# LayerNorm roots moved to GpSimd, and ScalarE's order changed, in the self-attention stage of a decoder block

## The chip, the cores and the metric

The kernel runs on one core of a Trainium2 chip. The metric is the device time of one execution, in microseconds (us). A core has five engines that run their own instruction streams and meet at semaphores: TensorE (PE, its weight loads PEld), VectorE (DVE), ScalarE (ACT), GpSimd (POOL) and SyncE (SP), which here issues the DMAs.

## What is computed

A decoder block: `x + attention(layernorm(x))`, then the same with cross-attention, then with a mixture of experts. The change touches the first of the three, causal self-attention with 16 heads over 16 sequences of 224 rows and 512 columns, whose softmax is replaced by a rational function:

```python
def rational_softmax(scores, eps=EPS):
    num = 0.5 * (1.0 + scores * jax.lax.rsqrt(1.0 + scores * scores))
    return num / (jnp.sum(num, axis=-1, keepdims=True) + eps)
...
def _layernorm(x, axis=-1, eps=1e-05):
    m = jnp.mean(x, axis=axis, keepdims=True)
    v = jnp.var(x, axis=axis, keepdims=True)
    return (x - m) / jnp.sqrt(v + eps)
```

## The kernel before

The stage works in NIT = 8 iterations of two sequences (448 rows, four tiles of 112). An iteration has NG = 8 slots, and a slot handles one group of four heads of one sequence. The bodies are called first (i = 0), second (1), mid (2 to 6, a loop) and last (7). Nothing is scheduled by a tool: each engine's `body` writes its instructions slot by slot, and a table `PLAN` says which matrix products (units) PE computes beside the attention in each slot. Precise products are made of float32 numbers split into a high and a low part, so every operand has a high part (ACT copies it) and a low part (DVE subtracts).

In slot s:

- **PE** (L853) makes `scores(s + 1)` (L799 to L815), then `values(s)` (L819 to L835, which waits for the weights' two halves and for `o_made` of slot s - 1), then the slot's units. Slot 0 has Q3, a transpose, OUT2 and OUT3; slot 1 has K3, V2, V3 and the transpose T1c0; slots 2, 3 and 4 are light (Z0 and Z1; Z2; Z3 and OUT0, and a transpose each); slots 5, 6 and 7 have three products each. OUT2 waits for `o_lo` of all eight slots of the iteration before. Products alternate between two PSUM banks.
- **ACT** (L690) takes the high part of the output of slot s - 1 (`hi_of_output`, L660), then `roots(s + 1)`: a square of the scores (L641), a reciprocal root (L643), a square (L645). Then `reciprocal(s)`, copies of PE's products out of PSUM (`evacuate`), and `off_diagonal(s + 1)` (L649). The square waits for the scores and for `y_made` of the slot before, since it overwrites what DVE then reads.
- **DVE** (L551) makes the low part of the output of slot s - 1 (L509), then `product_signed(s + 1)` (L486) and `numerator(s + 1)` (L490, L493, L495; `y_made` comes from L493), then `output(s)` (L501, L502, L504; it sets `o_made`), then low parts of transposes, residuals and LayerNorm statistics.

The two LayerNorms of an iteration, half 0 (the next rows of x) and half 1 (rows after attention), have their root in three pieces: DVE's statistics (`mv_made`), ACT's reciprocal root of four numbers per row (`root_of`, L597, 0.28 us) and five tiny DVE instructions that refine it (`refine`, L467 to L475). ACT then normalises the four tiles (`normalise`, L602). For half 0 the root is in slot 0 and the tiles are in slot 1, for half 1 they are in slots 1 and 2. Half 0's tiles are what T1c0 transposes in slot 1. SP loads the next rows and stores Z0 after half 1's tiles are done (`xn_made[1]`). POOL does nothing in the eight iterations.

Of the kernel before, what the change touches and what calls it, by code (L numbers as in the profile page):

```python
# [11 lines left out]
R = T // 2  # L12
TPI = 4
# [113 lines left out]
def self_attention(nc, ctx, block, handover, x, w_qkvT, w_outT, w_qT, slopes, x1_dram, q2_dram):  # L127
# [51 lines left out]
    nt = [sb(f"nt{k}", [R, 2, TPI]) for k in range(2)]  # L179
# [26 lines left out]
    newton = [sem("newton0"), sem("newton1")]  # L206
    rstd_made = [sem("rstd_made0"), sem("rstd_made1")]
# [86 lines left out]
    CONSTS = 6  # L294

# [86 lines left out]
    def _(pool):  # L382
# [15 lines left out]
        for a in range(2):  # L398
# [9 lines left out]
                           base=0, channel_multiplier=1).then_inc(const_ready, 1)  # L408

    @block.vector  # L410
    def _(dve):
# [177 lines left out]
        refine(1, NIT - 1)  # L589
# [4 lines left out]
    def _(act):  # L594
        def root_of(half, n):
            act.wait_ge(mv_made[half], n * TPI + TPI)
            act.activation(rstd[half][:], mv[half][:, :, 1], ACT.Abs_reciprocal_sqrt, bias=eps[0:R, 0:1]).then_inc(root_made[half], 1)  # L597

        def normalise(half, n, src, dst):
            act.wait_ge(rstd_made[half], n + 1)  # L600
            for j in range(TPI):
                ins = act.activation(dst[:, j, :], src[:, j, :], ACT.Identity, bias=shift[half][:, j:j + 1],  # L602
                                     scale=rstd[half][:, j:j + 1])
            ins.then_inc(xn_made[half], 1)
# [58 lines left out]
        root_of(0, 0)  # L663
# [15 lines left out]
        root_of(0, 1)  # L679
# [10 lines left out]
        def body(i, kind):  # L690
            for s in range(NG):
                if s > 0:
# [31 lines left out]
        root_of(1, NIT - 1)  # L724
# [1178 lines left out]
```

## Time and profile before

| | us |
|---|---|
| median of 3 runs (3229.09, 3233.4, 3235.1) | 3233.4 |
| the profiled execution, its own time | 3229.13 |
| its span, first to last instruction | 3227.3 |
| self-attention stage, until about | 765 |
| of an iteration (slot 0 at 304.55 to the next at 388.86) | 84.31 |

PE was busy 94% of the span, DVE 51%, ACT 42%, POOL 22%; the mean granted clock was 0.97. In the first stage PE is busy for 644.2 of 765 us and DVE for 584.4. A matmul's record has a modelled end, so a PE without gaps is read from its starts. Idle time in brackets in a row is that of the engine just before the instruction, with what ended it. In the names, `a_ew` holds the scores' work tiles, `a_o_sb` the output, `a_oTh` and `a_oTl` its high and low part.

### The profile page before, as it was taken

The page shows a single profiled execution, that of the slowest core. Times are in us where ns is not written, and L with a number is a line of the kernel's source. Part 1 is how long each engine was busy: PE and PEld are TensorE (multiplying, and loading weights), DVE is VectorE, ACT ScalarE, POOL GpSimd, SP SyncE. Part 2 cuts the span into 40 slices and gives each one's busy share as a digit, 9 for nine tenths or more (in the row PEclk, how much of TensorE's full clock was granted, in tenths as well). Part 3 has the DMA queues.
Part 4 walks back from the last instruction along what each step waited for, and adds up shares of the span by engine and source line. Part 5 has one row for each costly group of instructions (what it writes and reads, how often), then busy time and mean ns, then how long its engine had stood idle before and what let it go on. Part 6 is the DMA issues. An engine that isn't in the chain of part 4 may idle for free. (4 is left out here: it accounts for less than half of the span.)

```text
span 3227.3 us, 50841 instructions
## 1 busy us (share of the span) xinstructions
PE 3018.3 (94%) x19312; PEld 2477.8 (77%) x19312; DVE 1646.6 (51%) x3608; ACT 1348.0 (42%) x2298; POOL 700.2 (22%) x721
## 2 busy tenths in 40 slices
PE   5889998978999999999999949999999999999997
PEld 4667777756788777778777738888888888888886
DVE  5888888873556556666566633333333333333321
ACT  5677777764555555555555511111111111111111
POOL 0000000011111221112121033243434343434332
PEclk9889999989999999999999969999999999999999
DMA  3011111123111111111111022141313131313122
GB/s 100 24 35 44 37 45 45 46 82 121 42 50 38 45 38 56 51 38 42 41 52 34 25 74 75 54 97 55 96 55 96 56 95 56 95 57 94 57 71 37
DMA packets 93875, 189.72 MB, mean 59 GB/s; under 512 B 17568, under 2 KB 27552, under 8 KB 91712
## 3 DMA queue, kind: packets, MB, share of 16 engines
q1 hardware_dynamic: 79168, 158.68, 16.1%
q0 software_dynamic: 14592, 29.43, 5.1%
q8 instruction: 82, 1.34, 0.2%
q14 instruction: 33, 0.27, 0.0%
HBM read 140.25 MB, written 47.82 MB: 58 GB/s over the span
## 5 line engine op out<-in xcount | busy, mean ns | idle before, releaser
L1777 ACT ACTIVATE f_hf<-f_h 128x448 f32<-128x448 f32 x256 | 139.4, 544 | 1014.1 <-PE f_h L1804 958.0
L1748 DVE CAST f_hh<-f_hf 128x448 fp32r<-128x448 f32 x256 | 105.9, 414 | 847.0 <-ACT f_hf L1777 822.0
L1819 PE MATMUL f_y<-f_w2h,f_hh 128*128 128x512 f32 x896 | 357.5, 399 | 0.0
L1819 PE MATMUL f_y<-f_w2h,f_hl 128*128 128x512 f32 x896 | 354.0, 395 | 0.0
L1819 PE MATMUL f_y<-f_w2l,f_hh 128*128 128x512 f32 x896 | 352.2, 393 | 0.0
L1707 POOL TENSOR_TENSOR f_w1l<-f_raw,f_w1h 128x512 fp32r<-128x512 f32 x128 | 182.4, 1425 | 778.6 <-DVE f_w1h L1731 778.5
L1396 ACT ACTIVATE c_s_sb<-c_s_sb,c_nmx 112x750 f32<-112x750 f32 x256 | 236.1, 922 | 159.6 <-DVE c_nmx L1239 156.6
L1388 ACT COPY c_pT<-psum 125x672 f32<-125x672 f32 x256 | 184.6, 721 | 224.3 <-PE psum L1496 223.2
L1804 PE MATMUL f_h<-f_xTh,f_w1h 128*128 128x448 f32 x1024 | 255.2, 371 | 2.9 <-DVE f_xTl L1736 1.4
L1496 PEld LDWEIGHTS psum<-a_ident,c_s_sb 112*125 112x125 f32 x1536 | 193.5, 189 | 79.9 <-issue 76.2
L1804 PE MATMUL f_h<-f_xTl,f_w1h 128*128 128x448 f32 x1024 | 250.7, 366 | 0.0
L1804 PE MATMUL f_h<-f_xTh,f_w1l 128*128 128x448 f32 x1024 | 249.7, 365 | 0.0
L1235 DVE CUSTOM_DVE_ANT_0 c_s_sb<-psum,c_mb 112x750 f32<-112x750 f32 x256 | 238.5, 932 | 0.0
L1496 PE MATMUL psum<-a_ident,c_s_sb 112*125 112x112 f32 x1536 | 221.4, 280 | 6.5 <-ACT c_pT L1388 6.5
L1804 PEld LDWEIGHTS f_h<-f_xTh,f_w1h 128*128 128x128 f32 x1024 | 188.3, 188 | 50.8 <-DVE f_xTl L1736 23.2
L1487 PE MATMUL psum<-h_kT,h_q 64*112 64x376 f32 x1024 | 196.9, 502 | 13.1 <-DVE c_mx L1235 11.9
L1804 PEld LDWEIGHTS f_h<-f_xTh,f_w1l 128*128 128x128 f32 x1024 | 193.0, 189 | 16.8
L1804 PEld LDWEIGHTS f_h<-f_xTl,f_w1h 128*128 128x128 f32 x1024 | 192.8, 188 | 16.5
L1819 PEld LDWEIGHTS f_y<-f_w2h,f_hl 128*128 128x128 f32 x896 | 168.2, 188 | 39.6
L1819 PEld LDWEIGHTS f_y<-f_w2l,f_hh 128*128 128x128 f32 x896 | 169.0, 189 | 29.6
L1819 PEld LDWEIGHTS f_y<-f_w2h,f_hh 128*128 128x128 f32 x896 | 168.3, 188 | 29.3
L1191 POOL DMA_INDIRECT table_dram<-c_pay,c_slotu x64 | 61.9, 967 | 539.4 <-DVE c_slotu L1318 524.8
(252 smaller groups left out, 5766.6 us busy)
## 6 DMA issues: line engine op xcount, KB each, us to landing
f_raw<-in_w SPq DMA_DIRECT2D x128, 512.0 KB, 4.2
h_craw<-in_ctxT SPq DMA_DIRECT2D x16, 1125.0 KB, 5.1
a_x_in<-in_x SPq DMA_DIRECT2D x9, 896.0 KB, 5.5
a_xr<-in_x SPq DMA_DIRECT2D x8, 896.0 KB, 6.0
x_dram<-a_xr SPq DMA_DIRECT2D x8, 896.0 KB, 4.8
q_dram<-a_q SPq DMA_DIRECT2D x32, 224.0 KB, 5.4
h_q<-q_dram SPq DMA_DIRECT2D x16, 448.0 KB, 5.4
c_x<-x_dram SPq DMA_DIRECT2D x16, 448.0 KB, 4.9
```

Source lines behind the costliest of these rows:

```text
L1191: pool.indirect_dma_start(out=table_dram, out_offset=bass.IndirectOffsetOnAxis(ap=slotu[:, q:q + 1], axis=0), in_=pay[:, q, :], in_offset= ...
L1235: nc.vector.tensor_tensor_reduce(out=half(s_sb[:, h % 4, :]), in0=score_view(h), in1=half(mb[:]), scale=1.0, scalar=-FLT_MAX, op0=ALU.add, ...
L1388: act.copy(probs_view(h), pt_view).then_inc(p_copied, 1)
L1396: act.activation(s_sb[:, h % 4, :], s_sb[:, h % 4, :], ACT.Exp, bias=nmx[:, h:h + 1], accum_out=den[:, h:h + 1]).then_inc(e_made, 1)
L1487: mm = pe.matmul(scb[e][0:R, a, 0:HW], q[rows, m, t0:t0 + R], kT[rows, m, j0:j0 + HW], start=True, stop=True, tile_position=(64 * e, 0))
L1496: mm = pe.transpose(ptb[0:JB, 128 * j:128 * j + R], s_sb[:, h % 4, JB * j:JB * j + JB], ident[:])
L1707: pool.tensor_tensor(w1s[1][:, l % NSLOT].rearrange("p k c -> p (k c)"), raw1[:, g % 2, l % 2, :], w1s[0][:, l % NSLOT].rearrange("p k c - ...
L1748: dve.tensor_copy(hs[0][:, l % 2, c * HC:c * HC + HC], hf[:, c, :]).then_inc(h_hi, 1)
L1777: act.activation(hf[:, c, :], H[:, 0:HC], ACT.Gelu_apprx_tanh).then_inc(free, 1)
L1804: mm = pe.matmul(H[:, 0:HC], w1s[a][:, l % NSLOT, k, :], xT[l // FB % 2][b][:, k, c * HC:c * HC + HC], start=q + k == 0, stop=(q, k) == (2 ...
L1819: mm = pe.matmul(Y[t][:], hs[a][:, l % 2, 128 * t:128 * t + 128], w2s[b][:, l % NSLOT, :], start=j == 0 and q == 0, stop=last_of_expert(l) ...
```

## The change

The three pieces of each root become one chain of 14 tiny instructions on POOL, an initial guess by bit arithmetic and two steps of refinement, each waiting for the one before. `root_of` and `refine` leave the loops of ACT and DVE. Half 0's four tiles are normalised at the end of slot 0, half 1's at the ends of slots 1 and 2, two and two, each behind `off_diagonal`. ACT computes `roots(s + 1)` ahead of `hi_of_output(s - 1)`, and DVE makes `product_signed(s + 1)` ahead of the output's low part. The start of the stage and its end keep the old root.

```diff
+        def root_of_variance(half, use, mv_count, used_count):
...
+            pool.wait_ge(mv_made[half], mv_count)
+            pool.sem_inc(chain_seen, 1)
...
+            then(pool.tensor_scalar(var, mv[half][:, :, 1], LN_EPS, None, ALU.add))
+            then(pool.tensor_scalar(rows.bitcast(I32), var.bitcast(I32), -0.5, float(0x5f3759df), ALU.mult, ALU.add))
+            then(pool.tensor_tensor(square, rows, rows, ALU.mult))
+            then(pool.tensor_tensor(product, square, var, ALU.mult))
...
+            pool.tensor_scalar(shift[half][:], product, -1.0, None, ALU.mult).then_inc(rstd_made[half], 1)
+
+        def body(i, kind):
+            if kind in ("second", "mid"):
+                root_of_variance(0, i - 1, i * TPI + 2 * TPI, i + 1)
+            if kind != "first":
+                root_of_variance(1, i - 1, i * TPI, i - 1 if kind != "second" else None)
...
@@ DVE, body
                 late = [u for u in units(kind, s - 1, 1) if u[0] == "T"] if s > 0 else []
+                for unit in late:
+                    lo_of_transpose(i, kind, unit)
+                if has_step(kind, s + 1):
+                    product_signed(*step(i, s + 1))
                 if s > 0:
                     lo_of_output(i, s - 1)
                 elif kind != "first":
                     lo_of_output(i - 1, NG - 1)
-                for unit in late:
-                    lo_of_transpose(i, kind, unit)
                 if has_step(kind, s + 1):
-                    product_signed(*step(i, s + 1))
                     numerator(*step(i, s + 1))
-                if s == 0 and kind in ("second", "mid"):
-                    refine(0, i + 1)
-                if s == 1 and kind != "first":
-                    refine(1, i - 1)
                 output(i, s)
...
@@ ACT, body
+                if has_step(kind, s + 1):
+                    roots(*step(i, s + 1))
                 if s > 0:
                     hi_of_output(i, s - 1)
                 elif kind != "first":
                     hi_of_output(i - 1, NG - 1)
-                if has_step(kind, s + 1):
-                    roots(*step(i, s + 1))
-                if s == 0 and kind in ("second", "mid"):
-                    root_of(0, i + 1)
-                if s == 1 and kind != "first":
-                    root_of(1, i - 1)
                 reciprocal(i, s)
...
-                if s == 1 and kind in ("second", "mid"):
-                    normalise(0, i + 1, x_in, x_in)
-                if s == 2 and kind != "first":
-                    normalise(1, i - 1, xr, xn2)
                 if has_step(kind, s + 1):
                     off_diagonal(*step(i, s + 1))
+                if s == 0 and kind in ("second", "mid"):
+                    normalise(0, i + 1, x_in, x_in)
+                if s in (1, 2) and kind != "first":
+                    normalise(1, i - 1, xr, xn2, 2 * s - 2, 2 * s - 1)
                 for unit in late[1:]:
                     evacuate(i, kind, unit)
```

How the instructions stand, in the loop over the mid iterations. First ACT, from the end of slot 0 (the last instruction of `roots` is the row before these) into slot 1, before:

```order
L597 ACTIVATE a_rstd_102<-a_mv_100,a_eps 112x4 [waits a_mv_made0]
L653 ACTIVATE a_rden<-psum,a_eps 128x224 [waits a_pv_full]
L655 ACTIVATE a_rden<-a_rden 128x224 [waits a_rs_made]
L624 ISA
L626 ACTIVATE a_qT<-psum 128x448 [waits a_gen_full]
L609 CAST a_x2Th<-psum 128x448 [waits a_t_full]
L649 ACTIVATE a_ew<-a_ew 112x4x112 [waits a_y_made]
L660 CAST a_oTh<-a_o_sb 128x224 [waits a_o_made]
L637 REGISTER_ALU
L641 ACTIVATE a_ew<-psum 112x1344 [waits a_y_made,a_s_full]
```

and now, the same stretch:

```order
L701 CAST a_oTh<-a_o_sb 128x224 [waits a_o_made]
L694 ACTIVATE a_rden<-psum,a_eps 128x224 [waits a_pv_full]
L696 ACTIVATE a_rden<-a_rden 128x224 [waits a_rs_made]
L665 ISA
L667 ACTIVATE a_qT<-psum 128x448 [waits a_gen_full]
L650 CAST a_x2Th<-psum 128x448 [waits a_t_full]
L690 ACTIVATE a_ew<-a_ew 112x4x112 [waits a_y_made]
L640 REGISTER_ALU
L642 ACTIVATE a_x_in<-a_x_in,a_shift_106,a_rstd_102 112x512 [waits a_rstd_made0]
L642 ACTIVATE a_x_in<-a_x_in,a_shift_106,a_rstd_102 112x512 x3
L678 REGISTER_ALU
L682 ACTIVATE a_ew<-psum 112x1344 [waits a_y_made,a_s_full]
```

The output's high part has left the place ahead of the next square, and four normalised tiles have come there, which wait for POOL's chain.

Second DVE, the head of slot 0, before:

```order
L509 TENSOR_TENSOR a_oTl<-a_o_sb,a_oTh 128x224 [waits a_o_hi]
L485 ISA
L486 TENSOR_TENSOR a_ew<-psum,a_ew 112x1344 [waits a_r_made]
L490 SCALAR_TENSOR_TENSOR a_ew<-a_ew 112x1344 [waits a_rr_made]
L493 SCALAR_TENSOR_TENSOR a_ew<-a_ew 112x1344 [waits a_m_made,a_p_made]
L495 SCALAR_TENSOR_TENSOR a_ew<-a_ew,a_keep 112x4x224 [waits a_y_made]
L466 REGISTER_ALU
L467 TENSOR_TENSOR a_nt_104<-a_rstd_102 112x4 [waits a_root_made0]
```

and now:

```order
L529 TENSOR_TENSOR a_ew<-psum,a_ew 112x1344 [waits a_r_made]
L551 ISA
L552 TENSOR_TENSOR a_oTl<-a_o_sb,a_oTh 128x224 [waits a_o_hi]
L533 SCALAR_TENSOR_TENSOR a_ew<-a_ew 112x1344 [waits a_rr_made]
L536 SCALAR_TENSOR_TENSOR a_ew<-a_ew 112x1344 [waits a_m_made,a_p_made]
L538 SCALAR_TENSOR_TENSOR a_ew<-a_ew,a_keep 112x4x224 [waits a_y_made]
L543 REGISTER_ALU
L544 SCALAR_TENSOR_TENSOR a_dt<-psum,a_rden 128x224 [waits a_rden_made]
```

The low part, which OUT2 waits for, now stands behind the product of the next slot, and ahead of the instruction that sets `y_made`; the refinement is gone.

## Rows read from the trace of the kernel before

**Rows 1.** One iteration, busy time: us, each engine, granted clock, DMA share, GB/s
```profile
304.55:388.86 84.31, 77.29 (x689) 60.89 (x688) 69.89 (x103) 62.07 (x90) 0.00 (x0) 0.96 0.16 44
```
**Rows 2.** Waits in 100 to 600 us: us in total, times, longest
```profile
ACT a_oTh L660 <- DVE a_o_sb L504: 42.4, 24, 2.5
PE psum L832 <- DVE a_o_sb L504: 25.7, 12, 4.4
```
**Rows 3.** PE's timeline, first, third and fourth iteration: start, length, row, idle before
```profile
107.62 0.59 PE L832 MATMUL psum<-a_ew,a_v 112*32 112x224 f32 x8 [1.70 <-DVE a_o_sb L504]
...
264.30 0.58 PE L832 MATMUL psum<-a_ew,a_v 112*32 112x224 f32 x8 [1.81 <-DVE a_o_sb L504]
...
304.55 0.46 PE L807 MATMUL psum<-a_qT,a_kT 32*112 32x112 f32 x8
...
309.59 1.15 PE L737 MATMUL psum<-a_wouth,a_oTh 128*112 128x512 f32 x4
...
338.80 0.93 PE L832 MATMUL psum<-a_ew,a_v 112*32 112x224 f32 x8 [3.05 <-ACT a_ew L649]
...
348.62 0.58 PE L832 MATMUL psum<-a_ew,a_v 112*32 112x224 f32 x8 [2.91 <-DVE a_o_sb L504]
...
358.54 0.59 PE L832 MATMUL psum<-a_ew,a_v 112*32 112x224 f32 x8 [0.27 <-DVE a_o_sb L504]
```
**Rows 4.** ACT's and DVE's timeline in its slot 4
```profile
348.79 1.28 ACT L641 ACTIVATE a_ew<-psum 112x1344 f32<-112x1344 f32 x1
...
351.56 1.56 DVE L486 TENSOR_TENSOR a_ew<-psum,a_ew 112x1344 f32<-112x1344 f32 x1 [2.25 <-ACT a_ew L643]
353.03 1.55 DVE L490 SCALAR_TENSOR_TENSOR a_ew<-a_ew 112x1344 f32<-112x1344 f32 x1
354.69 1.56 DVE L493 SCALAR_TENSOR_TENSOR a_ew<-a_ew 112x1344 f32<-112x1344 f32 x1
356.28 0.58 ACT L649 ACTIVATE a_ew<-a_ew 112x448 f32<-112x448 f32 x1 [1.07 <-DVE a_ew L493]
...
358.71 1.28 ACT L641 ACTIVATE a_ew<-psum 112x1344 f32<-112x1344 f32 x1
```
**Rows 5.** Statistics of half 0, squares of slots 1 to 3, tiles of half 1
```profile
306.61 0.38 DVE L462 BATCH_NORM_AGGREGATE a_mv<-a_stats 112x2 f32<-112x6 f32 x4
...
316.48 1.28 ACT L641 ACTIVATE a_ew<-psum 112x1344 f32<-112x1344 f32 x1
...
328.14 1.29 ACT L641 ACTIVATE a_ew<-psum 112x1344 f32<-112x1344 f32 x1
...
335.32 2.92 ACT L602 ACTIVATE a_work<-a_xr,a_shift,a_rstd 112x512 f32<-112x512 f32 x4
...
338.88 1.28 ACT L641 ACTIVATE a_ew<-psum 112x1344 f32<-112x1344 f32 x1
```
**Rows 6.** The second stage: its chain of roots on POOL, DVE beside it
```profile
1009.73 0.22 POOL L1168 TENSOR_SCALAR c_nt<-c_mv 112x2 f32<-112x2 f32 x1 [4.32 <-DVE c_mv L1254]
...
1010.95 0.61 DVE L1225 TENSOR_SCALAR c_s_sb<-c_s_sb,c_rec 112x750 f32<-112x750 f32 x1
1011.27 0.36 POOL L1172 TENSOR_SCALAR c_nt<-c_nt 112x2 f32<-112x2 f32 x1 [0.20 <-POOL c_nt L1171]
...
1013.71 0.19 POOL L1178 TENSOR_SCALAR c_nt<-c_nt 112x2 f32<-112x2 f32 x1 [0.20 <-POOL c_nt L1177]
```
**Rows 7.** POOL beside DVE in the last iteration; durations min/median/max in ns
```profile
L94 POOL TENSOR_TENSOR h_wvl<-h_stage,h_wvh x3: 1272/1278/1441, 704.7 to 707.4; 128x512 fp32r<-128x512 f32 x3
...
705.30 0.95 DVE L504 SCALAR_TENSOR_TENSOR a_o_sb<-a_dt 128x224 f32<-128x224 f32 x1
...
L504 DVE SCALAR_TENSOR_TENSOR a_o_sb<-a_dt x64: 391/391/1653, 64.8 to 729.3; 128x224 f32<-128x224 f32 x64
```
**Rows 8.** Granted clock (third number from the end) in slot 4, two iterations
```profile
350.00:355.00 5.00, 5.00 (x31) 4.19 (x24) 3.34 (x3) 4.31 (x7) 0.00 (x0) 0.74 0.00 0
...
265.00:270.00 5.00, 5.00 (x43) 4.21 (x35) 2.76 (x2) 4.90 (x7) 0.00 (x0) 1.00 0.04 6
```

More of the change, by code:

```diff
@@ L178, in self_attention @@
     rstd = [sb(f"rstd{k}", [R, TPI]) for k in range(2)]
-    nt = [sb(f"nt{k}", [R, 2, TPI]) for k in range(2)]
+    nt = [sb(f"nt{k}", [R, 3, TPI]) for k in range(2)]
     shift = [sb(f"shift{k}", [R, TPI]) for k in range(2)]
@@ L206, in self_attention @@
     newton = [sem("newton0"), sem("newton1")]
+    chain, chain_seen = [sem("chain0"), sem("chain1")], sem("chain_seen")
     rstd_made = [sem("rstd_made0"), sem("rstd_made1")]
@@ L294, in self_attention @@
     CONSTS = 6
+    CHAIN = 13
     QKV_DEAD = (gen_full, product_number(NIT - 1, "last", "V3") + 1)
@@ L408, in _, with then @@
                            base=0, channel_multiplier=1).then_inc(const_ready, 1)
+        def root_of_variance(half, use, mv_count, used_count):
+            var, square, product = (nt[half][:, k, :] for k in range(3))
+            rows = rstd[half][:]
+            done = [0]
+            def then(ins):
+                done[0] += 1
+                ins.then_inc(chain[half], 1)
+                pool.wait_ge(chain[half], use * CHAIN + done[0])
+                pool.sem_inc(chain_seen, 1)
+            pool.wait_ge(mv_made[half], mv_count)
+            pool.sem_inc(chain_seen, 1)
+            if used_count is not None:
+                pool.wait_ge(xn_made[half], used_count)
+                pool.sem_inc(chain_seen, 1)
+            then(pool.tensor_scalar(var, mv[half][:, :, 1], LN_EPS, None, ALU.add))
+            then(pool.tensor_scalar(rows.bitcast(I32), var.bitcast(I32), -0.5, float(0x5f3759df), ALU.mult, ALU.add))
+            then(pool.tensor_tensor(square, rows, rows, ALU.mult))
+            then(pool.tensor_tensor(product, square, var, ALU.mult))
+            then(pool.tensor_scalar(square, product, -10 / 3, None, ALU.add))
+            then(pool.tensor_tensor(square, square, product, ALU.mult))
+            then(pool.tensor_scalar(square, square, 5.0, 3 / 8, ALU.add, ALU.mult))
+            then(pool.tensor_tensor(rows, square, rows, ALU.mult))
+            then(pool.tensor_tensor(square, rows, rows, ALU.mult))
+            then(pool.tensor_tensor(product, square, var, ALU.mult))
+            then(pool.tensor_scalar(product, product, -0.5, 1.5, ALU.mult, ALU.add))
+            then(pool.tensor_tensor(rows, product, rows, ALU.mult))
+            then(pool.tensor_tensor(product, mv[half][:, :, 0], rows, ALU.mult))
+            assert done[0] == CHAIN
+            pool.tensor_scalar(shift[half][:], product, -1.0, None, ALU.mult).then_inc(rstd_made[half], 1)
[4 more added lines that the diff above has]
+                root_of_variance(1, i - 1, i * TPI, i - 1 if kind != "second" else None)
+        iterations(pool, body)
     @block.vector
@@ L594, in _, with root_of, normalise @@
     def _(act):
-        def root_of(half, n):
-            act.wait_ge(mv_made[half], n * TPI + TPI)
+        def root_of(half, count):
+            act.wait_ge(mv_made[half], count * TPI)
             act.activation(rstd[half][:], mv[half][:, :, 1], ACT.Abs_reciprocal_sqrt, bias=eps[0:R, 0:1]).then_inc(root_made[half], 1)
-        def normalise(half, n, src, dst):
+        def normalise(half, n, src, dst, *js):
             act.wait_ge(rstd_made[half], n + 1)
-            for j in range(TPI):
+            for j in js or range(TPI):
                 ins = act.activation(dst[:, j, :], src[:, j, :], ACT.Identity, bias=shift[half][:, j:j + 1],
                                      scale=rstd[half][:, j:j + 1])
-            ins.then_inc(xn_made[half], 1)
+            if j == TPI - 1:
+                ins.then_inc(xn_made[half], 1)
         def hi_of_transpose(i, kind, unit):
@@ L662, in _ @@
         act.wait_ge(const_ready, CONSTS)
-        root_of(0, 0)
+        root_of(0, 1)
         for k in range(KC):
@@ L678, in _ @@
         roots(0, 0)
-        root_of(0, 1)
+        root_of(0, 2)
         for unit in ("V0", "V1"):
```

4 lines of the change are left out of this document (2 added, 2 removed).

## Prediction

> **What bounds the kernel now.** I read the busy times of one iteration first [rows 1]. Of 84.3 us PE is busy 77.3 and DVE 69.9: neither fills it, so the order of waits decides, slot by slot. The waits say where [rows 2]: ACT sits 42 us of 500 ahead of the output's high part, which waits for DVE, and PE 26 us ahead of `values`, for the same DVE instruction. Then PE's timeline [rows 3]: in the fourth iteration (i = 3, slot 0 at 304.55) PE waits 3.05 us in slot 3, 2.91 in slot 4 and 0.27 in slot 5, that is in and behind the light slots. In slots 5, 6, 7 and 0 it runs without a gap, and there the scores come so late that nothing ACT does sooner helps. So there are two regimes: heavy slots go by PE, light slots by a ring through ACT and DVE. I count all times from slot 0 of an iteration; the ring runs from the start of one square (call it R) to the next.
>
> **The ring, before and after.** In slot 4 one turn is 348.79 to 358.71, 9.92 us [rows 4]: square and root until DVE's product starts, 2.77; to the first half of the numerator 1.47; to its second half 1.66; to `y_made` 1.59; then the off-diagonal copy beside 0.8 us of DVE's third part and output, the output's high part, and the next square. The change takes the wait for the output out. ACT's next square then waits for `y_made` and the off-diagonal copy ahead of it, 0.5 us. But DVE's low part now stands inside the ring: it needs ACT's high part, which follows the third of the roots (product start + 1.33 + 0.38, less overlap), so it starts 1.66 us after the product did and takes 0.30: the numerator begins 0.5 us later than today. New turn: 2.77 + 1.96 + 1.65 + 1.59 + 0.52 = 8.5 us, 1.4 less. `o_made`, which PE's next `values` waits for, comes at R + 10.1; today it is R + 9.7 (348.79 to 358.5). So what one slot gives, the half microsecond takes back once at the end of the light stretch.
>
> **Removed from DVE and ACT.** Five refinements per half, some 0.2 us each, 2 us of DVE per iteration; ACT's 0.3 us root. In heavy slots DVE and ACT are idle beside PE and this is worth nothing; in slot 1 it takes 0.9 us from the way to `o_made`.
>
> **Added: the chain on POOL.** The nearest rows are the second stage's chain [rows 6]: the first instruction at 1009.73, the eleventh at 1013.71, less the 0.17 that one of them was held, so 0.38 us a step. Fourteen steps take 5.15 us when nobody disturbs them. Half 0's statistics are made at 2.4 (306.61 + 0.38 - 304.55) [rows 3, 5]; the half microsecond on DVE makes it 2.9, and the chain starts at 3.1. Undisturbed it ends at 8.3, before the tiles want it (off-diagonal copy done at 9.5).
>
> It will be disturbed. In the second stage a chain step of 0.19 us took 0.36, since a DVE instruction with 0.61 us was running: it ended 0.07 us after DVE's did [rows 6]. In the last iteration DVE's L504, whose two inputs both lie in SBUF, took 0.95 and once 1.65 us where its median is 0.39, both times beside POOL's subtractions, and one of POOL's three took 1441 ns where the others took 1272 and 1278 [rows 7]. So one of the two engines stands while the other runs, and it goes both ways. The Trainium skill states this ("SBUF — State Buffer", section "SBUF: two separate sides"): VectorE and GpSimd share a port pair under an exclusive lock, which a VectorE instruction with two SBUF inputs takes against a GpSimd instruction that reads SBUF. The trace agrees, by the 1441 ns and the 1.65 us. In this stage L490, L493 and L495 have two SBUF inputs and stand back to back for 4.2 us (the first two in [rows 4], the third is 1.09 long); L486 has one in PSUM and took nobody's time.
>
> Step by step: product at 3.8; by the low part's end, 5.8, eight steps are done. The ninth waits for L490 and ends at 7.5, the tenth for L493 (9.1), the eleventh for L495 (10.2), the twelfth at 10.6, the thirteenth behind L504 (11.3), the last at 11.7. The chain takes 8.6 us, not 5.15. My bounds are 8.3 (no holding) and 12.5 (POOL loses each turn to DVE's next instruction and only goes on behind L495); I take 11.7, because rows 6 and 7 both show the waiting engine getting its turn at the other's end.
>
> **Moved: the tiles of half 0.** ACT, done with the off-diagonal copy at 9.5, waits 2.1 us for the chain; four tiles are 2.92 [rows 5], of which 2.85 pass before the next. The square of slot 1 starts at 14.55. Today it starts at 11.93 (316.48) [rows 5], so the slot begins 2.6 us late, and queued behind the tiles on ACT are that square and PE's copies.
>
> From there by the new terms. `y_made` is R + 7.97 = 22.5; off-diagonal copy, two tiles of half 1 (1.4), a copy of V3 and of T1c0 (0.9): slot 2's square at 25.4; today 23.6. Half 1's chain starts at 15.0, runs mostly beside L486, ends by 22.7 and is not waited for. Slot 2: `y_made` 33.4, copy 0.5, two tiles 1.4: slot 3's square at 35.3; today 34.3. PE's `values` in slot 3 wait for `o_made` at 25.4 + 10.1 = 35.5; today 34.25. Slot 4: 35.3 + 10.1 = 45.5; today 44.1. `xn_made[1]` comes at 35.4, today 33.7: SP's queue behind it (next rows, the stores of Z0 to Z2) shifts by 1.7, and ACT's copy of Z2, which waits for Z0's store, starts at 42.5, so slot 4's square starts at 43.9, today 44.2. Slot 5's `values` start at the later of two: the ring's 43.9 + 10.1 = 54.0, and PE's own way through slot 4. Today they start at 53.99. PE's own way is 1.1 later (45.5 against 44.1, less the 0.27 it waits today) if PE runs slowly in slot 4, and earlier than 54.0 if it does not. In the iteration shown the granted clock over 5 us of slot 4 was 0.74, after a wait of 2.91 us; an iteration earlier it was 1.00, after 1.81 [rows 3, 8]. Full is 2.4 GHz, the lower level 1.2. Three of the five mid iterations are of the first kind. So a mid iteration costs 0 to 1.1 more: five make **+3.2**.
>
> **OUT2.** The output's low part of slot 7, the last that OUT2 waits for, now stands behind slot 0's product: it is there at 5.9, and OUT2 wants it at 5.04 (309.59) [rows 3]. PE waits 0.9 us in slot 0. In mid iterations this hides, since slot 1's square comes later than PE does, at 14.55 against 12.7. If the chain were fast it would still hide, because the tiles end at 12.4.
>
> **First, second, last.** In the first iteration there are no tiles and PE has little to do, so the ring is shortened without a price: PE's wait of 1.70 in slot 5 [rows 3] goes, and with the 1.4 us per turn in slots 3 and 4 it comes out **-2.3**, less what slots 5 to 7 of 10.0 us give back. The second pays the late tiles as a mid one does: **+0.8**. The last has no tiles of half 0 and gains in its light slots, with the loads that it waits for in slot 2 unmoved in kind: **-1.1**. Stages two and three are not touched.
>
> **Sum.** -2.3 + 0.8 + 3.2 - 1.1 = +0.6 us against the profiled execution's own 3229.1: 3229.7. That execution was 4.3 below the median of the runs, so on the median's scale about **3234 us**. A measurement of this kernel can tell about 0.2%, 6.5 us, from no change.
>
> **Rivals.**
>
> *The ring gets free* (chance 0.19). POOL's small steps slip between DVE's, or wait only for a short part of each. For it: no row shows a short POOL step beside L490 itself. Against: rows 7. The chain ends at 8.3, slot 1's square at 12.4, everything behind is 2.1 us earlier than above: a mid iteration gains 1.1 to 2.1, first and second 3.6, last 1.1: 12 us in all, 3221.
>
> *PE keeps its clock in the light slots* (0.05). If the waits of about 3 us fell under 2, as in the third iteration, slots 3 and 4 would lose nothing: up to 2 us an iteration beyond the above, some 14 us in all, 3220. Against: the waits worked out above are 3.2 and 3.1, not shorter.
>
> *The chain is the new bound* (0.18), on the other side. POOL gets no turn from L490 to L495 and DVE is in turn held by POOL's steps, 0.4 us a numerator. Slot 1's square then starts at 15.4 and the numerator is longer: 1.2 more in each of six iterations, 7 us, 3241. It decides from the point where the chain ends later than 9.5, since from there each us of it is one of ACT's. For it: the chain is 8.6 us in a gap of 6.4. Against: the two-way turns in rows 7.
>
> Main case, within 0.2%: 0.58. With a rest for clocks and runs: faster 0.24, same 0.58, slower 0.18. The range reaches from the free ring (3221) and the kept clock (3220) to the bound chain and its scatter, 3242.
>
> **What would show it.** In the page of the changed kernel: POOL steps in the first stage with a mean well over 0.2 us, up to 1.5 under L490 and L493; ACT waiting about 2 us for POOL ahead of the four tiles (if it waits under 0.3, the first rival holds); PE waiting about 0.9 us for `a_oTl` ahead of OUT2; ACT's wait for L504 ahead of the high part gone; squares 8.5 us apart in slots 3 and 4 of the first iteration; a mid iteration of 84.3 to 85.4 us. If it is under 83 or over 86 I am wrong, and the place is slot 1's square, at 14.55.

## The result and the profile after

| | before | after |
|---|---|---|
| median of the runs, us (12 each, same chip) | 3229.98 | 3238.44 |
| lowest and highest | 3227.68 to 3236.79 | 3236.76 to 3242.31 |
| profiled execution: time, span | 3229.1, 3227.3 | 3237.24, 3235.5 |
| granted clock, mean of the span | 0.970 | 0.968 |

The ratio is 1.0024, interval [1.0015, 1.0033]: the change costs 8 us. The time lies in the range, but not where the forecast put it (no difference within 0.2%): it is slower by a little more than that. A ratio is good to about 3 us either way, here and in the experiments below (4 us where a kernel had five to seven runs).

Where the 8.2 us between the two spans lie. The marks are the starts of the squares of each iteration's first group (L641 before, L682 after):

| stretch | before | after | difference | forecast |
|---|---|---|---|---|
| up to the first square | 40.88 | 41.33 | +0.4 | 0 |
| first iteration | 86.87 | 84.38 | -2.5 | -2.3 |
| second | 83.07 | 84.41 | +1.3 | +0.8 |
| five mid iterations | 422.51 | 425.34 | +2.8 | +3.2 |
| last, to its last square | 83.16 | 85.45 | **+2.3** | **-1.1** |
| from there to the second stage's first scores | 51.22 | 52.24 | +1.0 | 0 |
| second and third stage | 2459.59 | 2462.35 | **+2.8** | **0** |

The first three terms of the forecast are met within 0.6 us. The last iteration is missed by 3.4 us and the later stages by 2.8.

Waits of the kernel after, 100 to 600 us (columns: who waits, for whom; us in total, times, longest), the answer to [rows 2]:

```profile
DVE a_ew L529 <- ACT a_ew L684: 75.8, 46, 2.8
...
ACT a_ew L690 <- DVE a_ew L536: 49.2, 38, 2.4
PE psum L869 <- DVE a_o_sb L547: 37.6, 22, 4.3
...
ACT a_x_in L642 <- POOL a_shift L443: 13.9, 6, 2.4
...
PE psum L774 <- ACT a_kT L669: 5.6, 6, 1.1
PE psum L774 <- DVE a_oTl L552: 4.9, 6, 1.1
```

ScalarE's 42 us ahead of the output's high part are gone from the list. Its wait ahead of the off-diagonal copy, also for VectorE, has grown by 24 us; before, it was

```profile
ACT a_ew L649 <- DVE a_ew L493: 25.3, 27, 2.2
```

New are ScalarE's wait for the chain, PE's for the low part ahead of OUT2 (both forecast), and one that the prediction gave no price: PE waits for ScalarE's copy of K, which stands behind the late tiles.

GpSimd's chain of half 0 in the fourth iteration, VectorE beside it, and PE at OUT2 with ScalarE at the tiles (timeline after; start, duration), the answer to [rows 4, 5]:

```profile
307.17 0.23 POOL L429 TENSOR_SCALAR a_nt<-a_mv 112x4 f32<-112x4 f32 x1 [64.76 <-DVE a_mv L505]
...
308.74 0.22 POOL L433 TENSOR_SCALAR a_nt<-a_nt 112x4 f32<-112x4 f32 x1 [0.20 <-POOL a_nt L432]
309.14 0.20 POOL L434 TENSOR_TENSOR a_nt<-a_nt 112x4 f32<-112x4 f32 x1 [0.18 <-POOL a_nt L433]
309.54 0.33 POOL L435 TENSOR_SCALAR a_nt<-a_nt 112x4 f32<-112x4 f32 x1 [0.20 <-POOL a_nt L434]
310.06 1.29 POOL L436 TENSOR_TENSOR a_rstd<-a_nt,a_rstd 112x4 f32<-112x4 f32 x1 [0.18 <-POOL a_nt L435]
311.52 1.48 POOL L437 TENSOR_TENSOR a_nt<-a_rstd 112x4 f32<-112x4 f32 x1 [0.18 <-POOL a_rstd L436]
313.18 0.95 POOL L438 TENSOR_TENSOR a_nt<-a_nt 112x4 f32<-112x4 f32 x1 [0.18 <-POOL a_nt L437]
...
315.73 0.23 POOL L443 TENSOR_SCALAR a_shift<-a_nt 112x4 f32<-112x4 f32 x1 [0.20 <-POOL a_nt L441]
```
```profile
307.80 1.56 DVE L529 TENSOR_TENSOR a_ew<-psum,a_ew 112x1344 f32<-112x1344 f32 x1 [0.98 <-ACT a_ew L684]
309.43 0.39 DVE L552 TENSOR_TENSOR a_oTl<-a_o_sb,a_oTh 128x224 fp32r<-128x224 f32 x1
309.74 1.55 DVE L533 SCALAR_TENSOR_TENSOR a_ew<-a_ew 112x1344 f32<-112x1344 f32 x1
311.39 1.56 DVE L536 SCALAR_TENSOR_TENSOR a_ew<-a_ew 112x1344 f32<-112x1344 f32 x1
312.98 1.09 DVE L538 SCALAR_TENSOR_TENSOR a_ew<-a_ew,a_keep 112x896 f32<-112x896 f32 x1
```
```profile
309.96 1.15 PE L774 MATMUL psum<-a_wouth,a_oTh 128*112 128x512 f32 x4 [0.77 <-DVE a_oTl L552]
...
312.98 0.58 ACT L690 ACTIVATE a_ew<-a_ew 112x448 f32<-112x448 f32 x1 [1.96 <-DVE a_ew L536]
315.99 2.94 ACT L642 ACTIVATE a_x_in<-a_x_in,a_shift,a_rstd 112x512 f32<-112x512 f32 x4 [2.43 <-POOL a_shift L443]
318.83 1.27 ACT L682 ACTIVATE a_ew<-psum 112x1344 f32<-112x1344 f32 x1
```

Beside L529, which has an input in PSUM, a step of the chain takes about 0.20 us. Beside L533, L536 and L538, whose inputs all lie in SBUF, it takes 1.29, 1.48 and 0.95, and each of the three ends 0.05 or 0.06 us after VectorE's instruction. So the chain advances one step per VectorE instruction, and VectorE pays nothing that shows: the 13 times that L533 (L490 before) ran beside a chain it took 1549 to 1552 ns, the other 51 times 1546 to 1554. ScalarE waits 2.43 us, and slot 1's square starts 14.9 us after slot 0 (303.92, where PE's scores begin, to 318.83); forecast 14.55.

The last iteration, where the forecast had a gain (the chain of half 1, then ScalarE in slot 1):

```profile
659.88 0.23 POOL L429 TENSOR_SCALAR a_nt<-a_mv 112x4 f32<-112x4 f32 x1 [76.94 <-DVE a_mv L505]
...
668.64 0.23 POOL L443 TENSOR_SCALAR a_shift<-a_nt 112x4 f32<-112x4 f32 x1 [0.20 <-POOL a_nt L441]
```
```profile
668.90 1.52 ACT L642 ACTIVATE a_work<-a_xr,a_shift,a_rstd 112x512 f32<-112x512 f32 x2 [2.81 <-POOL a_shift L443]
670.33 0.56 ACT L671 COPY a_v<-psum 112x512 f32<-112x512 f32 x1
670.79 1.29 ACT L682 ACTIVATE a_ew<-psum 112x1344 f32<-112x1344 f32 x1
```

Half 1's chain, "not waited for" in the mid iterations, is waited for here: there are no late tiles of half 0 that would hold ScalarE up for as long. Slot 1's square to slot 2's takes 13.24 us where it took 10.80.

### The profile page after: what moved, and what is told of

It is laid out like the page before. It is cut to its first block and busy times, and to the rows that moved or that the text cites. A ratio compares the mean times of both kernels' runs of the same rounds, so it can differ in the third digit from the quotient of the medians.

```text
span 3235.5 us, 51170 instructions
## 1 busy us (share of the span) xinstructions
PE 3024.1 (93%) x19312; PEld 2479.4 (77%) x19312; DVE 1643.1 (51%) x3543; ACT 1345.1 (42%) x2285; POOL 772.8 (24%) x903
## 5 line engine op out<-in xcount | busy, mean ns | idle before, releaser
L1841 PEld LDWEIGHTS f_h<-f_xTh,f_w1h 128*128 128x128 f32 x1024 | 188.5, 188 | 51.2 <-DVE f_xTl L1773 23.5
L1524 PE MATMUL psum<-h_kT,h_q 64*112 64x376 f32 x1024 | 198.0, 505 | 13.5 <-DVE c_mx L1272 12.3
```

What stands on the lines that cost most here:

```text
L1524: mm = pe.matmul(scb[e][0:R, a, 0:HW], q[rows, m, t0:t0 + R], kT[rows, m, j0:j0 + HW], start=True, stop=True, tile_position=(64 * e, 0))
L1841: mm = pe.matmul(H[:, 0:HC], w1s[a][:, l % NSLOT, k, :], xT[l // FB % 2][b][:, k, c * HC:c * HC + HC], start=q + k == 0, stop=(q, k) == (2 ...
```

## Experiments

Twelve kernels. "Against before" is the ratio of medians to the kernel before, run beside it on the same chip. The chips differ between groups of runs, so medians of different groups are compared by these ratios. In the tables a **step n** is the time from slot n's square to the next slot's, in a mid iteration (the fifth, i = 4, unless two values are given).

### The parts one by one

`ring_only`: the kernel before, with this on ScalarE and, on VectorE, `lo_of_output` moved behind `product_signed` in the same way.

```
+                if has_step(kind, s + 1):
+                    roots(*step(i, s + 1))
                 if s > 0:
                     hi_of_output(i, s - 1)
                 elif kind != "first":
                     hi_of_output(i - 1, NG - 1)
-                if has_step(kind, s + 1):
-                    roots(*step(i, s + 1))
```

> The kernel before with one part of the change: roots ahead of the output's high part on ScalarE, the signed product ahead of the output's low part on VectorE. Roots by ScalarE and VectorE and the tiles' places as before. Theory 1 (late tiles cost what the shorter ring gives): without the late tiles the ring's gain stays. First iteration -2.3, each of the seven others about -1 in slots 3 and 4, so 6 to 10 us under the kernel before: about 3222, and a mid iteration of 83.2 to 83.8. Theory 2 (the ring takes back what it gives, since o_made comes at R + 10.1 where it was R + 9.7, and PE's clock falls): within 3 us of the kernel before, a mid iteration of 84.3 to 84.9.

`chain_only`: the kernel before with `root_of_variance` on GpSimd for both halves, and `root_of` and `refine` taken out of the iterations:

```
+        def body(i, kind):
+            if kind in ("second", "mid"):
+                root_of_variance(0, i - 1, i * TPI + 2 * TPI, i + 1)
+            if kind != "first":
+                root_of_variance(1, i - 1, i * TPI, i - 1 if kind != "second" else None)
...
-                if s == 0 and kind in ("second", "mid"):
-                    refine(0, i + 1)
-                if s == 1 and kind != "first":
-                    refine(1, i - 1)
```

> The kernel before with another part alone: both roots by GpSimd's chain of 14 steps, orders and the tiles' places as before. Theory 1: the chain ends 8.6 us after its start, at about 11.4 for half 0 and 23 for half 1, ahead of tiles wanted at about 17 and 28, so nobody waits for it; DVE loses nothing by the turns: 0 to 5 us under the kernel before. Theory 2 (DVE is held in turn, 0.4 us a numerator beside a chain): 4 to 7 us above it, and L490, L493 (as numbered before) with means 0.2 or more above their medians in slots 0 and 1.

`tiles_back`: the changed kernel with

```
+                if s == 1 and kind in ("second", "mid"):
+                    normalise(0, i + 1, x_in, x_in)
+                if s == 2 and kind != "first":
+                    normalise(1, i - 1, xr, xn2)
                 if has_step(kind, s + 1):
                     off_diagonal(*step(i, s + 1))
-                if s == 0 and kind in ("second", "mid"):
-                    normalise(0, i + 1, x_in, x_in)
-                if s in (1, 2) and kind != "first":
-                    normalise(1, i - 1, xr, xn2, 2 * s - 2, 2 * s - 1)
```

> The changed kernel with the tiles at their old places: half 0's four in slot 1, half 1's four in slot 2, ahead of the off-diagonal copy. Theory 1 (ScalarE's wait of 2.4 us for the chain and the tiles in slot 0 are what costs): slot 1's square starts at 12 and not 14.9, a mid iteration is 83 to 84 us, the whole 8 to 16 us under the changed kernel. Theory 2 (the wait is hidden by PE as the heavy slots are PE's): within 3 us of the changed kernel.

`last_old`: the changed kernel with

```
-                if s in (1, 2) and kind != "first":
+                if s in (1, 2) and kind in ("second", "mid"):
                     normalise(1, i - 1, xr, xn2, 2 * s - 2, 2 * s - 1)
+                if s == 2 and kind == "last":
+                    normalise(1, i - 1, xr, xn2)
```

> The changed kernel, except that in the last iteration alone half 1's four tiles stand together in slot 2. Theory 1 (the last iteration's loss is ScalarE's wait of 2.81 us for half 1's chain in slot 1): slot 1 is 10.4 to 10.8 us instead of 13.2, the whole 2 to 3.5 us under the changed kernel. Theory 2 (the loads of h_stage and xr hold slot 2 anyway): under 1 us, slot 2 longer by what slot 1 is shorter.

| | median, us | against before | step 0 | step 1 | step 2 | step 3 | step 4 | step 5 |
|---|---|---|---|---|---|---|---|---|
| before | | 1 | 10.83 | 11.65 | 10.74 | 9.91 | 9.93 | 10.40 |
| ring_only | 3227.92 | 0.9992 [0.9983, 1.0001] | 11.62 | 11.71 | 10.46 | 8.42 | 11.42 | 10.42 |
| chain_only | 3233.13 | 1.0005 [0.9996, 1.0014] | 10.62 | 11.71 | 10.77 | 9.92 | 9.92 | 10.37 |
| tiles_back | 3231.37 | 1.0002 [0.9993, 1.0011] | 11.68 | 11.72 | 10.46 | 8.42 | 11.39 | 10.46 |
| last_old | 3236.51 | 1.0018 [1.0009, 1.0027] | 13.80 | 10.72 | 9.86 | 8.66 | 9.62 | 11.15 |
| after | 3238.44 | 1.0024 [1.0015, 1.0033] | 13.81 | 10.72 | 9.85 | 8.42 | 11.49 | 10.46 |

The parts add up within the intervals: ring and chain alone give 0.9992 and 1.0005, both with the tiles at their old places 1.0002. What is left, 1.0024 against 1.0002, is the tiles' move: 7 us, nearly the whole loss. `tiles_back` is nearer theory 1, but short of its 8 to 16 us below the changed kernel. Its mid iterations are 83.9 to 85.1 us, one of five under 84, and slot 1's square starts 12.8 us after slot 0, not 12: with the tiles gone from there, PE's wait ahead of OUT2 is bare.

`ring_only` is nearer theory 2: 2.4 us under the kernel before, and its mid iterations are 84.9 to 86.0 us (before: 84.3, once 85.2), while its first iteration gained 2.6. Two things take the ring's gain back. Step 0 is 0.8 to 0.9 longer, in every iteration but the first: PE's wait ahead of OUT2,

```profile
PE psum L738 <- DVE a_oTl L509: 4.9, 6, 1.1
```

(waits of `ring_only`, 100 to 600 us). And step 4 is longer: 11.4 us, in two of the five 12.4, for 9.9. Windows of i = 2 and 3, one line per step 3 and step 4 (columns: window, length, busy us and instructions of PE, PEld, DVE, ACT, POOL, granted clock, DMA share, GB/s):

```profile
251.94:260.36 8.42, 5.31 (x68) 4.28 (x68) 5.55 (x6) 6.47 (x10) 0.00 (x0) 1.00 0.63 165
260.36:272.74 12.38, 10.60 (x84) 8.05 (x88) 10.61 (x16) 6.52 (x11) 0.00 (x0) 0.72 0.24 59
...
337.96:346.37 8.41, 6.81 (x68) 5.51 (x68) 5.59 (x6) 6.47 (x10) 0.00 (x0) 0.80 0.65 172
346.37:357.80 11.43, 9.65 (x84) 7.71 (x88) 10.54 (x16) 6.47 (x11) 0.00 (x0) 0.85 0.24 54
```

PE still waits in the light slots, 3.05 us in slot 3 for the off-diagonal copy and 3.2 to 4.7 in slot 4 for the output, and around slot 4 its clock is at the lower level for a while. Before, that time lay in a step that the ring made 9.92 long anyway: there, too, PE was busy 9.65 of 9.92 us at a mean clock of 0.83. With a ring of 8.42 the step behind is PE's own: 84 matmuls take 9.65 at a mean clock of 0.85 and 10.60 at 0.72, and the step follows. In `tiles_back` the same step was 9.87 and 9.68 in two iterations where PE ran at 1.00 in it (the slower stretch lay in slot 3), and 11.39 to 11.46 in the other three, at 0.85. Step 5 gives a part back: it is 10.4 behind a slow step 4 and 10.9 to 11.1 behind a fast one. That the clock sets the length of step 4 is read from such rows; no run changes the clock alone.

`chain_only` answers the third rival. The chain at its old places is waited for by nobody, and steps 0 to 5 are as before, step 0 even 0.2 shorter (the refinements). Theory 2, VectorE held, is out: no step in the table is longer by more than 0.06. Yet the run is no faster (its interval reaches from 1.3 us faster to 4.5 slower); that is taken up below.

`last_old`: slot 1's square to slot 2's is 10.41 in the last iteration (13.24 after), as theory 1 says, and from that iteration's slot 0 to its last square it takes 72.0 us where the changed kernel takes 75.0, so slot 2 does not take it back. The whole is 1.9 us less, just under the 2 to 3.5 expected and too little to tell from the scatter; the step itself is what shows it.

### OUT2's wait, and the low part's place

`slot0_old`: `ring_only` with, on ScalarE,

```
+                if s == 0 and kind != "first":
+                    hi_of_output(i - 1, NG - 1)
                 if has_step(kind, s + 1):
                     roots(*step(i, s + 1))
                 if s > 0:
                     hi_of_output(i, s - 1)
-                elif kind != "first":
-                    hi_of_output(i - 1, NG - 1)
```

and the same for `lo_of_output` and `product_signed` on VectorE.

> The run ring_only, except that slot 0 alone keeps the old order on both engines (high part ahead of the roots, low part ahead of the product). In ring_only slot 0's square to slot 1's square took 11.68 where before it took 10.83. Theory 1 (the 0.85 is PE's wait ahead of OUT2 for the low part, no longer covered by late tiles): that step is 10.83 again in seven iterations, and the whole 4 to 6 us under ring_only, about 3222. Theory 2 (the light slots wait for the output anyway and PE's clock falls for as long): the 0.85 comes back in slots 3 to 5, within 2 us of ring_only.

`lo_late`: in addition, on VectorE:

```
                 if has_step(kind, s + 1):
                     product_signed(*step(i, s + 1))
+                if s == 4:
-                if s > 0:
                     lo_of_output(i, s - 1)
                 if has_step(kind, s + 1):
                     numerator(*step(i, s + 1))
...
                 output(i, s)
+                if s not in (0, 4):
+                    lo_of_output(i, s - 1)
```

> The run slot0_old, and the output's low part on VectorE goes behind output's three instructions in slots 1, 2, 3, 5, 6 and 7 (in slot 4, where OUT0 wants it, it stays behind the product). Theory 1 (from a square to the output was 10.19 because the low part and the late product stand in it): it is about 9.3, the wait of PE ahead of values in slots 3 and 4 is some 0.5 to 0.9 shorter, and the whole 3 to 8 us under slot0_old. Theory 2 (PE's way through slot 4 at its lower clock decides): within 2 us of slot0_old.

`tb_lo_late`: the orders of `lo_late` put into `tiles_back`.

> The same orders as lo_late, with GpSimd's chains and the tiles at their old places. Theory 1 (the chain is worth nothing where nobody waits for it, as chain_only at 3233 against 3230): within 3 us of lo_late. Theory 2 (without refinements on VectorE slot 1's output comes sooner, and it is that which the shorter ring can use): 3 us or more under lo_late.

`late_fixed`: the orders of `lo_late` put into the changed kernel, tiles late as they are.

> The changed kernel, chain and late tiles as they are, with the orders of lo_late (slot 0 as before the change, the output's low part behind the output in six slots). Theory 1 (the late tiles and the wait for the chain cost the same 7 us in any order): about 3225, 7 above tb_lo_late, with slot 0's square to slot 1's at 13.5 to 13.8. Theory 2 (with the output sooner PE has room, and the late tiles are hidden): within 3 us of tb_lo_late, 3218.

| | median, us | against before | step 0 | step 1 | step 3 | step 4 | mid iterations, us |
|---|---|---|---|---|---|---|---|
| slot0_old | 3224.57 | 0.9972 [0.9961, 0.9983] | 10.63 | 11.86 | 8.41 | 9.95 | 83.0 to 84.2 |
| lo_late | 3216.55 | 0.9952 [0.9938, 0.9965] | 10.63 | 11.87 | 7.96 | 11.42 | 82.9 to 85.0 |
| tb_lo_late | 3218.34 | 0.9956 [0.9942, 0.9969] | 10.62 | 11.71 | 8.31 | 9.53 | 82.7 to 84.7 |
| late_fixed | 3234.39 | 1.0011 [1.0002, 1.0019] | 13.72 | 11.52 | 8.23 | 11.14 | 83.5 to 85.4 |

`slot0_old`: the wait for `a_oTl` is gone from the list and step 0 back at 10.6; 0.9972 against `ring_only`'s 0.9992 is 6.5 us. Theory 1. `lo_late`: 6.5 us more by the ratios, which is theory 1 by the time, though by half of what was expected in the rows: from slot 3's square to the output that PE waits for it is 9.7 us and not 10.2 (9.3 was expected), PE's wait in slot 4 is 1.6 or 2.7 us in four iterations of five (4.2 in one) where `slot0_old` has 2.0 or 3.1, and that in slot 3, for the off-diagonal copy, is 3.05 as it was. It beats the kernel before by 15 us and the changed one by 23, with no root moved. `tb_lo_late` is within 2 us of it, less than the scatter: where nobody waits for it, the chain is worth nothing that can be measured (theory 1).

`late_fixed` met neither theory: 1.0011 against 0.9956 is 18 us, not 7 and not 3, though slot 0's square to slot 1's is 13.5 to 13.7, as theory 1 has it. With OUT2's wait gone PE only arrives sooner at the next: its products in slot 1 want a bank that ScalarE frees with K's copy, and that stands behind the tiles and a square. PE's timeline in slot 1, i = 3:

```profile
318.26 1.08 PE L776 MATMUL psum<-a_wqkvh,a_xTl 128*112 128x512 f32 x4
321.13 1.23 PE L776 MATMUL psum<-a_wqkvh,a_xTh 128*112 128x512 f32 x4 [1.79 <-ACT a_kT L671]
322.16 1.91 PE L776 MATMUL psum<-a_wqkvl,a_xTh 128*112 128x512 f32 x4
323.87 1.86 PE L776 MATMUL psum<-a_wqkvh,a_xTl 128*112 128x512 f32 x4
```

The wait is 1.79 us (1.0 in the changed kernel), and behind it four matmuls take 1.9 us instead of 1.08: the lower clock. In a mid iteration where the clock stayed up, step 1 took 10.26; in the four others 11.52. That is a part of the 18 us: in the profiled executions the two kernels' mid iterations differ by 1.6 us on the mean, and the first stage by 13.6 us; the later stages of that execution of `late_fixed`, the fastest of its twelve, are 3.4 shorter. The rest is not followed.

### The price of waiting for the chain

`short_chain`: the changed kernel without the last refinement,

```
-    CHAIN = 13
+    CHAIN = 9
...
-            then(pool.tensor_tensor(square, rows, rows, ALU.mult))
-            then(pool.tensor_tensor(product, square, var, ALU.mult))
-            then(pool.tensor_scalar(product, product, -0.5, 1.5, ALU.mult, ALU.add))
-            then(pool.tensor_tensor(rows, product, rows, ALU.mult))
```

> The changed kernel with four of the chain's fourteen steps left out, the second refinement of the root: the roots are coarser, nothing else differs. Theory 1 (ScalarE's wait of 2.4 us for the chain is on the path of slot 0): the wait is under 0.5, slot 0's square to slot 1's is 11.7 to 12.4 and not 13.8, and the whole 4 to 10 us under the changed kernel. Theory 2 (the late tiles alone cost what they cost, by PE's copies behind them): within 2 us of the changed kernel.

3231.03 us, 0.9998 [0.9989, 1.0007]: 8 us under the changed kernel by the ratios. Step 0 is 12.01 (13.81), ScalarE waits 0.6 us at most (under 0.5 was expected; waits, 100 to 600 us):

```profile
ACT a_x_in L638 <- POOL a_shift L439: 3.1, 5, 0.6
```

Theory 1. The 1.8 us that step 0 gets back are worth 2.2 in the second iteration, 2.4 in the last (half 1's chain: 11.45 for 13.24) and 0.3 to 2.2, 0.9 on the mean, in a mid one, where step 1 takes up the rest (11.49 for 10.72).

This and `tiles_back` say together what the late tiles cost. Steps 0 and 1 of a mid iteration sum to 22.5 us before, 24.5 in the changed kernel, 23.5 in `short_chain` with the tiles late, and 23.4 in `tiles_back` with the whole chain. So of the 2 us one is ScalarE's wait for the chain. The other is PE's wait ahead of OUT2, which `ring_only` has too (23.3 to 23.4) and `slot0_old` not (22.5). The tiles' new place by itself costs nothing as long as that wait stands beside them.

### Why the second stage is longer

In `chain_only` the first stage got 1.5 us shorter between first and last square, and the kernel did not get faster. That is within its interval, but the second stage has a loss of the same size that repeats. In the second stage the twelve periods from the 25th scores to the 121st (the matmuls of L1487 before) took 816.2 to 816.5 us in the five kernels without the chain (`ring_only`, `slot0_old`, `lo_late` and the two below), and 817.8 to 818.6 in all seven with it (before: 817.7, with two longer steps of another kind, told below). The difference comes in equal pieces, 0.13 us in each period, at one place: the fifth of a period's eight intervals between scores is 6.45 instead of 6.32. The kernel `lo_late`, then `tb_lo_late`, there (timeline, start and duration):

```profile
1002.46 0.19 ACT L1399 ACTIVATION_READ_ACCUMULATOR c_s_sb<-c_s_sb,c_nmx 112x1 f32 x1
...
1002.70 0.19 POOL L1181 TENSOR_SCALAR c_nt<-c_nt 112x2 f32<-112x2 f32 x1 [0.20 <-POOL c_nt L1180]
1002.77 0.16 DVE L1226 RECIPROCAL c_rec<-c_den 112x1 f32<-112x1 f32 x1 [1.18 <-PE psum L1499]
```
```profile
1002.77 0.19 ACT L1435 ACTIVATION_READ_ACCUMULATOR c_s_sb<-c_s_sb,c_nmx 112x1 f32 x1
...
1003.02 0.19 POOL L1217 TENSOR_SCALAR c_nt<-c_nt 112x2 f32<-112x2 f32 x1 [0.20 <-POOL c_nt L1216]
...
1003.22 0.16 DVE L1262 RECIPROCAL c_rec<-c_den 112x1 f32<-112x1 f32 x1 [1.31 <-PE psum L1535]
```

ScalarE and GpSimd stand to each other as before; VectorE's reciprocal starts 0.20 after GpSimd's step instead of 0.07. Nothing of this stage was edited. Three kernels asked what else moved. `wide_nt` and `more_sems` are `lo_late` with one of these each:

```
-    nt = [sb(f"nt{k}", [R, 2, TPI]) for k in range(2)]
+    nt = [sb(f"nt{k}", [R, 3, TPI]) for k in range(2)]
...
+    chain, chain_seen = [sem("chain0"), sem("chain1")], sem("chain_seen")
```

`dve_shift` is `tb_lo_late` with

```
+        for cell in cells:
+            dve.memset(cell, 0.0)
         dve.wait_ge(x_loaded, 16)
```

with 34 one-column places of `stats[1]`, `mv[1]` and `shift[1]` as `cells`.

> The run lo_late with the scratch of both roots one row larger, as in the change, and not used. In every run with GpSimd's chain in the first stage the second stage is longer: one RECIPROCAL of VectorE per period starts 0.19 us after a GpSimd step began, at that step's end, where without the chain it starts 0.06 after it; the period is 0.13 longer, some 2 us over the stage. Theory 1 (the places of the second stage's tensors in SBUF, which the larger scratch moves, decide it): 0.19 here as well. Theory 2 (it is not the places): 0.06 and the period of lo_late.

> The run lo_late with the three semaphores of the change allocated and not used, so that the second stage's semaphores have other numbers. Theory 1 (the numbers decide the 0.13 us): the reciprocal starts 0.19 after the GpSimd step. Theory 2: 0.06, as in lo_late, and what is left is GpSimd's own program.

> The run tb_lo_late (GpSimd's chain, tiles at their old places, orders of lo_late) with 34 small memsets at VectorE's very start, where it waits for its first load. The chain took 34 instructions out of VectorE's program ahead of the second stage's loop and put 88 into GpSimd's; the memsets put VectorE's loop back at the count it has before the change. Theory 1 (where VectorE's loop lies in its program decides the 0.13 us by which the RECIPROCAL of every period starts late): it starts 0.06 after the GpSimd step again, and the second stage, from the first scores to the 126th, is 1066 us and not 1068.4; the whole 1 to 3 us under tb_lo_late. Theory 2 (it is GpSimd's program, or that both engines take part): 0.19 as before, and the time of tb_lo_late within 1.5 us.

`wide_nt`, a single execution: 3212.49 us, reciprocal 0.06 after the step, twelve periods in 816.2. `more_sems`, a single execution: 3212.87 us, 0.07 and 816.3. So it is neither the tensors' places nor the semaphores' numbers. `dve_shift`: 3219.94 us, 0.9947 [0.9933, 0.9960] (its chip ran the kernel before at 3238.17, so the ratio counts; it is not to be told from `lo_late`'s and `tb_lo_late`'s).

```profile
999.01 0.19 POOL L1220 TENSOR_SCALAR c_nt<-c_nt 112x2 f32<-112x2 f32 x1 [0.20 <-POOL c_nt L1219]
999.07 0.17 DVE L1265 RECIPROCAL c_rec<-c_den 112x1 f32<-112x1 f32 x1 [1.18 <-PE psum L1538]
```

0.06 again, and the 0.13 is gone from every period: with GpSimd's chain and its program unchanged, 34 instructions ahead of VectorE's loop undo it. That is theory 1 for the place; how a loop's place acts on this one instruction no run shows. Its times were not met: 1071.4 us to the 126th scores, not 1066, since in nine of the twelve periods another interval, which is 9.22 in `lo_late`, took 9.84 to 9.89, so that this kernel's twelve periods are the longest of all, 822.1. Before has two such, `tb_lo_late` none. What makes that one come and go stays open.

Because of its two, the profiled kernel before takes 817.7 us for the twelve periods and the changed one 817.8: the 0.13 us are no part of the +2.8 in the table above. Of that, 1.2 us lie ahead of the 25th scores, 1.4 between the 126th and the last, and 0.3 behind. Among the fourteen kernels' profiles the first stretch takes 204.8 to 208.4 and the second 14.6 to 17.4, so a single pair says nothing of a cause there. Not tried: shifting GpSimd's program alone.

## Why the prediction was right where it was, and wrong where not

**The chain's length: right, with one step miscounted.** Forecast 8.6 us from start to end; measured 8.79 (307.17 to 315.96). It ended 12.04 us after slot 0, forecast 11.7 with bounds of 8.3 and 12.5. The mechanism is the one argued from [rows 6, 7]: a step runs to the end of VectorE's instruction and gets its turn there. The Trainium skill ("SBUF — State Buffer", section "SBUF: two separate sides") calls the shared port pair an exclusive lock that holds for a whole instruction, and the rows agree: about 0.20 us beside an input in PSUM, 1.29 and 1.48 beside two in SBUF. The turn between two VectorE instructions is in the rows. What the prediction had wrong is "by the low part's end, 5.8, eight steps are done": from 3.1 on, eight steps of 0.38 us end at 6.1, so seven are done. The trace has seven, and the eighth (L436) waits where the ninth was expected. That one step is the 0.34 us by which the chain ended late. The first rival (a free ring) is out, the chain is 8.8 us and not 5.15. Half of the third (VectorE held 0.4 us a numerator) is out too: L533 beside a chain takes what it takes without.

**Slot 1's square and the squares behind it: right.** Forecast, counted from slot 0: 14.55, 25.4, 35.3, 43.9; measured 14.9, 25.7, 35.5, 44.3. `values` of slots 3, 4 and 5: forecast 35.5, 45.5 and 54.0 to 55.1, measured 35.9, 45.7 and 54.5. The waits: ScalarE 2.1 forecast, 2.43 measured; OUT2 0.9 forecast, 0.77.

**The mid iterations: right in sum, with the shares a little off.** +3.2 forecast, +2.8 measured; 84.4 to 85.6 each, forecast 84.3 to 85.4. The bound of 0 to 1.1 for PE's clock was the right form: the steps 4 of 9.5 to 9.9 (clock 1.00) and of 11.3 to 11.5 (0.85) are the two cases. But two iterations were of the slow kind and not three, at 85.6, and the three fast ones were 84.4 to 84.9 and not 84.3. That these two misses cancel is luck.

**OUT2: right here, wrong in what was said of it in general.** The text says the wait would hide even with a fast chain, since the tiles end at 12.4. By its own numbers it would not quite: PE comes at 12.7. In `short_chain`, where ScalarE still waits 0.6 us, slot 1's square starts at 13.12 and PE's scores are ready at 12.75, so it hides by 0.4. It hides only behind the late tiles: in `tiles_back` PE's scores set the square, at 12.8. There the same wait costs about 1 us an iteration: 0.9992 to 0.9972 for removing it.

**The last iteration: the failed step.** "The last has no tiles of half 0 and gains in its light slots": -1.1 forecast, +2.3 measured. I carried "half 1's chain is not waited for" from the mid iterations to this one. There it starts at 319.04 and the tiles are wanted 8.2 us later; here it starts at 659.88 and they are wanted at 666.09, 6.2 later, since no late tiles of half 0 hold ScalarE up. The chain took 7.8 us in the one place and 9.0 in the other; even in the mid iteration it was done only 0.4 us ahead of its tiles (326.83). Here ScalarE waits 2.81 us; `last_old` takes the step from 13.24 to 10.41. And OUT2's wait is bare: slot 0's square to slot 1's is 11.68 where it was 10.70. The two steps are 3.4 us longer than before, the size of the error.

**The second stage: a term that was not there.** "Stages two and three are not touched" was taken as zero. Every kernel with the chain and no padding pays 0.13 us a period, 1.5 us in twelve, by the place of VectorE's loop. It is within the scatter of the stage and no part of the +2.8 of the profiled pair, which lies at the stage's two ends and whose cause stays open.

**On the verdict.** By its mechanism the loss is that of the third rival's second condition, "each us past 9.5 is one of ACT's", without its first (VectorE held). The forecast had put the price of that at zero net, because the first and last iterations were to pay for it. The first did. Had the last been sized right, the sum would have been +4: still within 0.2%, but with more of the chance on the slower side.

**Luck.** The range, 3220 to 3242, is wide enough to hold a gain of 13 us as well as a loss of 8, so the time lying in it says little for the mechanism; the squares and waits above say more. And it was built on a median of 3233.4 for the kernel before, from three runs, where the twelve gave 3230.0. The measured ratio on the old median would be 3241.2, within 1 us of the end of the range. The main case, no difference within 0.2%, was missed.

## What to carry to other kernels

When a ring is shortened, find the result that other engines wait for, and ask what is placed ahead of it: here the low part stood ahead of the output by habit of order, and moving it behind was worth 6.5 us, where moving every root to GpSimd was worth nothing that could be measured. Before a chain of small dependent steps goes to GpSimd, count which instructions of VectorE run beside it: here the price was one of them per step while their inputs all lay in SBUF, and it was paid by the engine that waited for the chain. And work each kind of iteration by itself: a wait that is covered in the middle ones was bare in the last.

## What the runs showed of the hardware that was not expected

- With steps this short the wait is one-sided. Beside L533 to L538 GpSimd's steps of 0.2 us grew to as much as 1.6, and VectorE's instruction took 1549 to 1552 ns with a chain beside it and 1546 to 1554 without. With GpSimd instructions of 1.3 us VectorE was held too [rows 7].
- A stage that nobody edited changed by 0.13 us in every period of 68: one instruction starts 0.06 to 0.07 or 0.19 to 0.20 us behind a GpSimd step, by 34 instructions more or fewer ahead of the loop in VectorE's program (one kernel with padding, five runs, one profile).
- With PE's granted clock, small shifts become large ones: in the same program, step 4 took 9.5, 11.4 or 12.7 us (`lo_late`), at mean clocks of 1.00, 0.85 and 0.73. Step 5 gives 0.8 us of it back, and mid iterations of one execution still differ by up to 2.1 us (82.9 to 85.0), more than most of the changes tried here gave in one.
